# Key windows of 32 rows with 96 more under a predicate, three staging buffers and stores from ScalarE in the attention of a graph network

## What is computed

```python
h = layernorm(triplet_h, ln_attn_g, ln_attn_b)
qkv = (h @ Wqkv + bqkv).reshape(n, 3, H, DH)          # H = 8 heads, DH = 32
q = qkv[:, 0] * SCALE; k = qkv[:, 1]; v = qkv[:, 2]
scores = jnp.einsum('ehd,ehd->eh', q[src], k[dst])
m = jax.ops.segment_max(scores, dst, num_segments=n)
e = jnp.exp(scores - m[dst])
s = jax.ops.segment_sum(e, dst, num_segments=n)
he = (v[src] * (e / s[dst])[:, :, None]).reshape(-1, D)
agg = jax.ops.segment_sum(he, dst, num_segments=n)
```

## Time and profile before

| what | us or share |
|---|---|
| median of 3 runs | 7011.9 |
| lowest and highest run | 6974.3, 7047.2 |
| the profiled execution, its own time | 7004.8 |
| its span | 7003.0 |
| VectorE busy | 3675.3 (52%) |
| GpSimd (POOL) busy | 3244.6 (46%) |
| TensorE (PE) busy | 2900.5 (41%) |
| ScalarE (ACT) busy | 1725.5 (25%) |
| moved by DMA | 1066.0 MB, mean 152 GB/s |
| SP's queue q1, POOL's queue q0 | 595.7 MB, 466.3 MB |
| granted clock of TensorE, mean | 0.69 |

### The profile page before, as it was taken

The page is one execution under the profiler, slowest core; times in us unless marked ns, Lnnn a source line. Parts: engine busy times, 40 slices in busy tenths (PEclk is TensorE's granted clock), DMA queues, the critical chain, the costliest instruction groups (busy, mean ns, idle before and its releaser), DMA issues. The chain is left out here.

```text
span 7003.0 us, 50568 instructions
## 1 busy us (share of the span) xinstructions
PE 2900.5 (41%) x12855; PEld 1680.4 (24%) x12907; DVE 3675.3 (52%) x8221; ACT 1725.5 (25%) x4386; POOL 3244.6 (46%) x3188
## 2 busy tenths in 40 slices
PE   4352001533354555699000597000300045677658
PEld 3211000311132222344000243000200024555435
DVE  8995444465555656444554433333543354565553
ACT  2270000122224555211232221323300022232222
POOL 0004776456536665100777301767277644555540
PEclk9696555755577777799555798555655567888879
DMA  0004554344434444233556433545255436878730
GB/s 8 1 1 148 184 187 161 101 153 168 157 109 140 160 161 151 94 153 139 178 195 208 167 134 136 197 168 193 92 181 193 167 131 203 270 260 276 248 98 19
DMA packets 379867, 1066.01 MB, mean 152 GB/s; under 512 B 74258, under 2 KB 162612, under 8 KB 333012
## 3 DMA queue, kind: packets, MB, share of 16 engines
q1 hardware_dynamic: 213586, 595.68, 22.6%
q0 software_dynamic: 164688, 466.32, 22.5%
q10 hardware_dynamic: 1330, 0.99, 0.0%
HBM read 541.40 MB, written 521.29 MB: 152 GB/s over the span
## 5 line engine op out<-in xcount | busy, mean ns | idle before, releaser
L790 POOL DMA_INDIRECT out_of<-table,index x936 | 966.5, 1033 | 706.6 <-DVE index L813 415.0
L790 POOL DMA_INDIRECT rows<-table,index x728 | 739.7, 1016 | 404.3 <-issue 217.4
L790 POOL DMA_INDIRECT rows<-typed_table,index x520 | 517.8, 996 | 587.2 <-DVE index L813 387.5
L3082 POOL DMA_INDIRECT qv<-qv_table,index x416 | 429.6, 1033 | 392.6 <-DVE index L3259 264.3
L790 POOL DMA_INDIRECT y<-typed_table,index x312 | 325.2, 1042 | 571.0 <-DVE index L813 462.7
L1460 PE MATMUL bank<-x,marks 128*128 128x416 f16 x1664 | 392.4, 400 | 315.2 <-ACT marks L1473 237.1
L825 DVE SCALAR_TENSOR_TENSOR y<-y,by_source_anew,out_of 128x256 f32<-128x256 f32 x897 | 436.4, 486 | 101.1 <-DMA out_of<-table,index 61.3
L1473 ACT ACTIVATE marks<-hot_block,x 128x128 f16<-128x128 f16 x1248 | 369.9, 386 | 346.0 <-DVE marks L1520 335.5
L2126 PE MATMUL bank<-weights,turned_y 128*128 128x512 f32 x800 | 357.5, 596 | 6.2 <-ACT turned_y L2186 5.5
L1933 PE MATMUL bank<-weights,out_of 128*128 128x512 f32 x800 | 349.7, 595 | 12.9 <-DVE weights L1978 12.9
L807 ACT ACTIVATE rows<-rows,by_target_weight 128x256 f32<-128x256 f32 x520 | 214.9, 494 | 518.8 <-DMA rows<-typed_table,index 270.0
(11 more groups left out here) (586 smaller groups left out, 7152.0 us busy)
## 6 DMA issues: line engine op xcount, KB each, us to landing
states<-y SPq DMA_DIRECT2D x156, 1024.0 KB
typed_table<-staged SPq DMA_DIRECT2D x400, 256.0 KB, 2.0
states<-state SPq DMA_DIRECT2D x78, 1024.0 KB
states<-out_of SPq DMA_DIRECT2D x78, 1024.0 KB
wide_states<-y SPq DMA_DIRECT2D x52, 1088.0 KB
near<-k_rows SPq DMA_DIRECT2D x416, 128.0 KB
out_of<-table,index POOLq DMA_INDIRECT x936
rows<-table,index POOLq DMA_INDIRECT x728
```

Source lines behind the costliest of these rows:

```text
L790: pool.indirect_dma_start(out=rows[h][:, u * D:(u + 1) * D], out_offset=None, in_=table, in_offset=bass.IndirectOffsetOnAxis(ap=index[h][: ...
L3082: pool.indirect_dma_start(out=qv[b][:, u * PAIR:(u + 1) * PAIR], out_offset=None, in_=qv_table, in_offset=bass.IndirectOffsetOnAxis(ap=ind ...
```

## The change

It has four parts. In `attention_pass` a window is moved in two pieces: its first `NEAR` = 32 rows always, rows 32 to 127 by a DMA with a predicate, `cond=wide`, which is skipped where the flag is 0 (its semaphore still rises). `wide` is one flag for each group, worked out by four more VectorE operations in `StepOrder.ahead`: 1 where a step of the group has more than 32 distinct targets. The stores are split in the same way. Fetches are issued by pairs of steps, each waiting only for the expansion of the pair that it replaces, with a semaphore for each pair and buffer. The stores move from SP to ScalarE: two for the first 32 rows (the early and the late half of the group) and a predicated one for the other 96; the staging buffers become three. `near` is set to zero at the start, and rows 32 to 127 of `wide_states` are set to zero by 13 DMAs during the permutation by source, so that everything that is read was written. To make room, two of the four `hot` buffers, `mark` and `score` move to borrowed memory.

```diff
-def permute(nc, env, blk, stp, piece, tiles, group):
+def permute(nc, env, blk, stp, piece, tiles, group, blanked=None):
...
+        blank = buffer(stack, nc, "blank", 4 * ROW)
...
+            if blanked is not None:
+                far = blanked[NEAR * STEPS:, :].rearrange("(l k u) d -> k l u d", k=STEPS // 32, u=32).rearrange("k l (j u) d -> k l j (u d)", u=4)
+                @block.gpsimd
+                def _(pool):
+                    pool.memset(blank[:], 0.0).then_inc(emptied, 1)
+                @block.sync
+                def _(sp):
+                    sp.wait_ge(emptied, 1)
+                    for k in range(STEPS // 32):
+                        sp.dma_start(far[k], blank[0:P - NEAR, :].unsqueeze(1).broadcast_to([P - NEAR, 8, 4 * ROW])).then_inc(stored, 16)
+                    sp.wait_ge(stored, 16 * (STEPS // 32))
...
         nc.vector.tensor_tensor(out=self.window[:], in0=total[:], in1=env.bank[4][:, 0:STEPS], op=ALU.add).then_inc(settled, 1)
+        dve.wait_ge(settled, 1)
+        then(nc.vector.tensor_tensor(out=quiet[:], in0=total[:], in1=self.window[:], op=ALU.subtract))
+        then(nc.vector.tensor_tensor(out=quiet[:], in0=quiet[:], in1=env.bank[3][:, 0:STEPS], op=ALU.add))
+        then(nc.vector.tensor_scalar(out=quiet[:], in0=quiet[:], scalar1=float(NEAR), scalar2=None, op0=ALU.is_ge))
+        then(nc.vector.tensor_reduce(out=self.wide, in_=bulk(quiet[:], GROUPS_T), axis=AX.X, op=ALU.max))
...
                 def fetch(g, h):
-                    for u in range(FEW):
-                        row = sp.value_load(steps.window[0:1, g * FEW + u:g * FEW + u + 1], min_val=0, max_val=ROWS - 1)
-                        sp.dma_start(near[h][:, u * D:(u + 1) * D], k_rows[bass.ds(row, P), :]).then_inc(windowed[h], 16)
-                def store(g, h):
-                    sp.wait_ge(kept, (g + 1) * FEW)
-                    sp.dma_start(blocks[:, g * (FEW * ROW):(g + 1) * (FEW * ROW)], staged[h]).then_inc(stored[h], 16)
...
+                    _, rows = nc.values_load_multi_w_load_instructions(
+                        steps.window[0:1, g * FEW:(g + 1) * FEW], engines=[mybir.EngineType.SP], min_val=0, max_val=ROWS - 1,
...
+                    wide = sp.value_load(steps.wide[0:1, g:g + 1], min_val=0, max_val=1)
+                    for k in range(PAIRS):
+                        if g >= 2:
+                            sp.wait_ge(expanded, 4 * (g - 2) + k + 1)
+                        for u in (2 * k, 2 * k + 1):
+                            sp.dma_start(near[h][0:NEAR, u * D:(u + 1) * D], k_rows[bass.ds(rows[u], NEAR), :]).then_inc(windowed[h][k], 16)
+                        for u in (2 * k, 2 * k + 1):
+                            sp.dma_start(near[h][NEAR:, u * D:(u + 1) * D], k_rows[bass.ds(rows[u] + NEAR, P - NEAR), :], cond=wide
+                                         ).then_inc(windowed[h][k], 16)
...
                 def expand(g, b, k, i):
-                    if k == 0:
-                        pe.wait_ge(windowed[h], (uses(i, b, 2) + 1) * (16 * FEW))
+                    pe.wait_ge(windowed[h][k], (uses(i, b, 2) + 1) * 64)
...
+                def store(g, steps_of):
+                    lo, hi = steps_of[0] * ROW, (steps_of[-1] + 1) * ROW
+                    act.wait_ge(kept, FEW * g + steps_of[-1] + 1)
+                    nc.scalar.dma_start(blocks[0:NEAR, g * (FEW * ROW) + lo:g * (FEW * ROW) + hi], staged[g % KEPT][0:NEAR, lo:hi]
+                                        ).then_inc(stored[g % KEPT], 16)
+                def store_wide(g):
+                    wide = act.value_load(steps.wide[0:1, g:g + 1], min_val=0, max_val=1)
+                    nc.scalar.dma_start(blocks[NEAR:, g * (FEW * ROW):(g + 1) * (FEW * ROW)], staged[g % KEPT][NEAR:], cond=wide
+                                        ).then_inc(stored[g % KEPT], 16)
...
                 def do(g, b, i):
                     spread_mark(g, b)
                     if at_least(g, 2):
-                        keep_sums(g - 2, b - 2, i, early)
+                        keep_sums(g - 2, early)
                     if at_least(g, 1):
                         raise_scores(g - 1, b - 1)
                     if at_least(g, 2):
-                        keep_sums(g - 2, b - 2, i, late)
+                        store(g - 2, early)
+                        keep_sums(g - 2, late)
                     if below(g, GROUPS_T - 1):
                         keep_hot(g + 1, b + 1)
                     keep_marks(g, b)
+                    if at_least(g, 2):
+                        store(g - 2, late)
+                        store_wide(g - 2)
...
+                for h in range(2):
+                    nc.vector.memset(near[h][:], 0.0).then_inc(blanked, 1)
                 for b in range(RING):
                     look(b, b)
```

More of the change, by code:

```diff
@@ L2591 @@
 MANY = 3
+NEAR = 32
+PAIRS = FEW // 2
+KEPT = 3
 class StepOrder:
```

87 lines of the change are left out of this document (43 added, 44 removed).

## The result

The changed kernel took 7060.7 us (median of 20 runs, 7002.6 to 7129.4) where the kernel before, timed beside it, took 7011.1: a ratio of 1.0071, interval 1.0049 to 1.0093. It is 49 us slower; the forecast was 84 us faster. The profiled execution of the changed kernel took 7002.6 us, the fastest of the 20, so its sum is not that of the median. Set beside the profiled execution before (7004.8 us), its stages are: everything up to the first window's matmul 33 us shorter although it holds the zeroing (5799.0 against 5831.6 us, so passes that the change doesn't touch moved by over 40 us between two executions), the first three groups 2.6 us longer, the 46 steady groups 24 us longer (760.9 against 736.8), the rest 3.5 us longer.

What follows compares the result with a forecast made beforehand. No engine near full; in `attention_pass` late `near` fetches and a slow stretch under POOL's gathers set the pace. -97 + 3.5 + 2 + 5 + 2.2 = -84 us on 7004.8: 6921, as median 6928 us; range 6830 to 7050.

Steps and rivals of the forecast that it cites:

- The near wait and the pair of groups: `attention_pass`, engines' chain: with `near` in time a pair of groups costs 9.85 + 16.6 us, 13.2 a group.
- POOL's slow stretch: While POOL issues indirect DMAs unpaused in the pass, semaphores and other sequencers slow down; adds SP 3.3 us a group.
- the crawl: Later name for POOL's slow stretch: the near standstill while POOL gathers without a pause; the prediction kept it.
- Bytes: A group's traffic in the pass falls from 4.2 to 2.6 MB, 8.1 us of DMA time, share 0.55 to 0.6.
- traffic rival: Traffic in the pass makes much of the crawl; fewer bytes give 11.2 us a group, 6804 us; chance 0.19.
- SP: SP's issuing in the pass needs 13.0 us a group, bounds 9.9 to 16.2, below the chain; skipped transfer 0.58.
- ScalarE: Its added stores and flag load in the pass put 0.7 us a group on the path, 1.9 with no cover.
- slower rival: ScalarE's added instructions at 0.7 us each in the crawl: 17.3 us a group, 7085 us; chance 0.11.
- SP as the bound: Skipped DMAs at the upper price give 16.2 us a group, 7034 us; chance 0.28, shared with partly uncovered blanking.
- Blanking: Zeroing 43.5 MB takes 126 us, hidden under the 164 us permutation, so 0; prediction wrong if that lasts over 165.
- Start and end of the pass: In `attention_pass`, memsets 3.5 us and issue about 2 at the start; 5 us, from 0 to 15, at the end.
- `StepOrder`'s 2.2 us: Four dependent VectorE operations added in `StepOrder`: 2.2 us, from 0 to 7.

Runs made afterwards that it cites:

- queues_only: Changed kernel with its queues kept but every transfer moving all 128 rows, without conditions, flags or zeroing: 6196.6 us, 0.9862 of the kernel before (chip 6).
- no_skipped: Changed kernel without its predicated fetches, predicated stores and flag loads: 6191.0 us, 0.9857 of the kernel before (chip 2).
- blank_early: Changed kernel with 4 of the 13 zeroing transfers issued one phase earlier: 6181.8 us, 0.9855 of the kernel before (chip 5).
- the spaced kernel before: Kernel before with GpSimd's gathers spaced, each two from the third on waiting for an earlier multiplication: 6836.2 us, 0.9890 on chip 11.

## Why the prediction was wrong, point by point

- **The near wait and the pair of groups: the step that failed.** The prediction took 9.85 + 16.6 us a pair with `near` in time, "this keeps POOL's slow stretch", and so 13.2 us a group. That subtracts a wait of 3.85 us from the first group of the pair and leaves the second as it is. It also set one pair against the mean of all: the pair of the earlier trace rows takes 30.3 us, 15.2 a group, and not the mean 16.0, so the same working on equal terms, 80.6 us of `near` waits less 46 x 0.7 for ScalarE, would have been 48 us and not 97. On the first chip the wait lay in a stretch in which PE, ScalarE and SP are late anyway. With it gone the first group did end 10.15 us after its start, as worked out, but the second started earlier, met the crawl with more work left and grew from 16.6 to 24 us: 16.5 us a group where 13.9 was forecast, 46 x 2.6 = 121 us of the miss. The rule was in the prediction's own reading (the crawl lasts as long as POOL is backlogged) and wasn't applied to the sum: what ends a pair there is the end of the burst and the work that remains behind it. That a wait lies beside gathers doesn't make it free by itself: of the `near` waits over 0.5 us, 75 of 77 us lay in POOL's runs on the first chip and 91 of 92 on chip 5, where their removal paid in full.
- **The same step on a chip without the crawl came out right in size.** 46 groups x 2.1 us were forecast, 46 x 2.3 us measured on chip 5, and the whole came to 82 us where the sum said 84. That is mostly chance: the trace read was one with the crawl, the two levels were 16.0 and 13.9 where these are 13.2 and 10.9, and the mean was set against one pair, as said.
- **Bytes: right that they are no bound**, also where the share is 0.95 (queues_only). The forecast share of 0.55 to 0.6 was 0.56. The traffic rival fell: 161 GB/s with the crawl in full, 308 GB/s with less of it, and 143 GB/s without gathers and without crawl.
- **SP: right that it isn't the bound, its terms were too high.** Lines of the changed kernel on chip 5:

```profile
L3130 SPq FUSED_REGOPS  x369: 156/156/166, 5347.9 to 5847.1; - x185
L3130 SPq MOVE near<-k_rows x369: 29/29/29, 5348.1 to 5847.3; - x185
L3130 SPq DMA_DIRECT2D near<-k_rows x369: 84/84/88, 5348.1 to 5847.4; - x185
```

  A skipped transfer costs 0.084 + 0.156 + 0.029 us and gaps, an estimate of 0.3 to 0.4 us, not 0.58. Leaving all of them out changed nothing without the crawl (no_skipped); with it, PE's steady waits name `near` nowhere.
- **ScalarE: 0.7 us on the path was forecast, at most 0.3 found** in the undisturbed group (10.15 against 9.85). The forecast's slower rival priced its added instructions at 0.7 us each in the crawl. The traces refute that price: each takes the same on the first chip as on chip 5, 0.28 us for the load and 0.33 for a store. Whether the stores cost something there in another way, by the order in which ScalarE takes up its waits, isn't settled, since no run separated stores and fetch on such a chip. That rival's own sum isn't clean either: 3.5 us on top of 13.2 makes a group of 16.7 us and 7057 us in all; its 17.3 counts the 0.7 twice. Its time, 7085 us, and that of SP as the bound, 7034, were nearer to 7061 than the forecast; both for a mechanism that the traces speak against.
- **Blanking: the mis-sized term.** 126 us from queue q1's 345 GB/s in the pass, measured 173: the zeroing ran at 252 GB/s and stuck out by 9 to 18 us (first gathers in its three traces at 590.3, 592.1 and 598.0 us, in those of the kernel before at 579.5 and 581.6). The prediction named 165 us for the phase as its own breaking point; it lasted 174.
- **Start and end of the pass:** 2.6 us at the start on the first chip (5.5 forecast with the memsets), 3.5 at the end (5 forecast). `StepOrder`'s 2.2 us can't be told from what else moves between two executions.

What stays open: why some chips show the crawl. The traces tie it to GpSimd's indirect DMAs (equal times up to the first one and in the long stretches without them) and, less firmly, to their spacing (0.9890), not to the bytes; they don't show what the sequencers wait for. Also open is what makes the changed kernel slower on such chips by 0.5 to 0.7%: the zeroing is worth 0.15% of it (a first gather 10 us later); for the rest there is the account above, of a covered wait and a longer second group. The traces on both such chips show it (on chip 11 too, 12 of the 46 groups take under 10.3 us and the ones behind them 21 on average), but no separate run proves it. And no one version was shown best on both kinds: 0.9855 for blank_early without the crawl, 0.9890 for the spaced kernel before with it; the spaced kernel with the new fetch had no run there.

## What to carry to other kernels

A wait that a profile shows is worth its length only if nothing else holds the same time: lay the waits of the path beside the stretches in which all engines stand, and move the whole pair of groups, not the one group. A high DMA share is no bound by itself; here it went from 0.95 to 1.04 while the kernel became faster, because the transfers were asked for earlier. And time the kernel before on more than one chip before you trust a reading of stalls that "issue" names: a change that pays 1.4% on one chip, and in its main parts on three more, lost 0.5 to 0.7% on two others.

## What the runs showed of the hardware

The same program took 6272 to 6281 us on four chips, and 6909 and 7011 us on two others. The difference begins with GpSimd's first indirect DMA, and in 316 us without gathers, at 143 GB/s of plain DMAs, it doesn't grow at all. On the slow chips register instructions of 18 to 152 ns on SP take about 700 ns for parts of a run of gathers, and PE and ScalarE come 3 to 8 us late, while ScalarE's own register and DMA instructions keep their times (medians of 277 against 278 and 328 against 328 ns) and POOL's unspaced gathers take 1.03 to 1.05 us, no more than the 1.05 to 1.10 us elsewhere. A fetch that its condition skips costs its issuer 84 ns for the DMA instruction, where one that moves 32 rows takes 326. And 43.5 MB of zeros from one small tile ran at 252 GB/s, less than the 386 GB/s that gathers, windows and stores reached together.
